# Segment maximum: two rows summed by matrix products with the identity, the maximum with zero taken in ScalarE's copy

## The chip, the core and the metric

The kernel runs on one core of a Trainium2 chip. The metric is the device time of one execution in microseconds, the median of several. A core has five engines with queues of their own: TensorE (PE, matrix products), VectorE (DVE), ScalarE (ACT), GpSimd (POOL) and SyncE (SP). DMA transfers are issued by SP, ACT and POOL. An instruction that has to wait for a semaphore holds up everything behind it on its own engine.

## The reference, cut to what matters

Four graph layers are applied to 12500 nodes of 64 features, with 400000 edges sorted by target node. The change is in the second layer, which computes an MLP on each edge and takes the maximum over the edges of each target:

```python
h = jnp.maximum(_layernorm(x, axis=-1), 0.0)
x_i = x[dst]; x_j = x[src]                     # x here is h
edge_features = jnp.concatenate([x_i, x_j - x_i], axis=-1)
h = jax.nn.relu(edge_features @ W1 + b1)
edge_messages = h @ W2 + b2
out = jax.ops.segment_max(edge_messages, dst, num_segments=x.shape[0])
```

The first product is split by linearity: every node gets one row that serves as a source (`tab1`) and one that serves as a target (`own1`, with the bias). For an edge, the hidden row is the maximum with zero of source row plus target row.

## The kernel before, in words

`target_maximum` handles the 400000 edges as 128 runs of 3125 consecutive edges, one run for each partition. It goes over them in 125 chunks (g) of 25 columns (`CB`), so a chunk is 25 edges on each partition, 128x1600 numbers. `by_columns` unrolls six chunks in a loop body; k is the place in it, so buffers are k % 2 or k % 3. Each engine runs its own list of stages, and `stage(f, lag, ...)` says which chunk a stage works on relative to g.

For a chunk:

- POOL (`gathers`) issues 25 indirect DMAs, one for each column, which bring the source rows into `G` (three buffers). Between them it issues 10 indirect DMAs that scatter records to `rec`; these belong to the later layers and only use this loop as a place to run. SP loads the source numbers (`idx`), the target rows and flags, and what the scatters need.
- ACT (`node_part`) writes target rows into `Xv`, which is laid out with features outside and columns inside (26 numbers from one feature to the next). DVE (`spread`) then carries the rows forward over the edges of one target by two scans. This is done one chunk ahead.
- DVE (`add`) sums `Xv` and `G` into `z`; ACT (`hidden`) takes the maximum with zero into `zr`.
- PE (`turn`) transposes `zr` in pairs of columns into `ps_t`, in four rounds of at most four pairs (4, 4, 4 and 1 pair; `NR2` is 4). ACT (`copies`) copies each round to `zT`, and PE (`messages`) multiplies it by the weights into `ps_m`.
- ACT (`messages`) copies `ps_m` into `Mv`, again with features outside; DVE (`scan`) takes the running maximum, and ACT (`turned`) turns it into `So`, which SP stores.

The names of instructions in the profile: `PT` is the lent memory that holds `Ein`, `G`, `Xv` and `rb`; `ACC` and `H` hold `z`, the two buffers of `zr`, and `Mv`. So "DVE ACC<-PT L1357" is the sum, "ACT ACC<-ACC L1434" and "H<-ACC L1434" are the maximum with zero. POOL's indirect DMAs have line 912 (gathers) and 891 (scatters) in this layer and in `target_attention`, the layer before it, whose loop has the same form with 15 scatters in a chunk; there the index tile is `t_idx`, here it is `m_idx`. POOL may start the gathers of chunk g when the chunk g - 3 has been read.

Of the kernel before, what the change touches and what calls it, by code (L numbers as in the profile page):

```python
# [37 lines left out]
def at_least(eng, sem, value):  # L38

    if not isinstance(value, int) or value > 0:  # L40
        eng.wait_ge(sem, value)
# [109 lines left out]
def settle(eng):  # L151


    eng.nop(nofuse=True)
# [18 lines left out]
def program(nc, x, src, dst, ea16, ea64, rowvec, wtab0, w_e, wtab1, w2, wtab2, watt_e, wgru, bgru, w1, w3, out):  # L173
# [11 lines left out]
    with ExitStack() as top:  # L185
# [713 lines left out]

            return r * (COLS_U // slots) + (k // slots + 1)  # L900

        def gathers(pool, G, table, idx, s_i, s_free, s_g, steps_in, g, k, r):

            q = k % 3
            pool.wait_ge(s_i[q], used(k, r, 3) * 16)
            at_least(pool, s_free, g - 2)
            settle(pool)
            at = {CB * (i + 1) // (steps_in.per + 1): i for i in range(steps_in.per)}
            for c in range(CB):
                if c in at:  # L910
                    steps_in.scatter(pool, at[c], k, r)
                pool.indirect_dma_start(G[:, q, c, :], None, table,  # L912
                                        bass.IndirectOffsetOnAxis(ap=idx[:, q, c:c + 1], axis=0)).then_inc(s_g[q], 16)
# [344 lines left out]
        def target_maximum():  # L1258
# [3 lines left out]
            NR2 = len(rounds)  # L1262
            with phase() as ctx:
                Mv = [hw[:, q * D * CW:(q + 1) * D * CW] for q in range(2)]
                zr = [accw[:, 2 * D * CW + CB * D:2 * D * CW + 2 * CB * D].rearrange("p (c d) -> p c d", c=CB),
                      hw[:, 2 * D * CW:2 * D * CW + CB * D].rearrange("p (c d) -> p c d", c=CB)]
                z = accw[:, 2 * D * CW:2 * D * CW + CB * D].rearrange("p (c d) -> p c d", c=CB)
                So = sb_in(ctx, "m_So", [P, 2, CB, D])
                w = sb_in(ctx, "m_w", [2 * D, 2 * D])
                zT = sb_in(ctx, "m_zT", [P, 2, 512])  # L1270
# [4 lines left out]
                ps_m = ps_in(ctx, "m_ps_m", [P, 2048])  # L1275
                ps_f = ps_in(ctx, "m_ps_f", [P, 1024])
                flags_in = ps_f[:, 0:HD * CW].rearrange("p (d c) -> p d c", c=CW)
                (s_w, s_wz, s_set, s_first, s_xv, s_F, s_Fm, s_R, s_car, s_z, s_zr, s_t, s_zT, s_msg, s_mv, s_S, s_cs, s_So) = (sem_in(ctx, "m_" + n) for n in (
                    "weights", "weights_zero", "edges_set", "first_rows", "node_rows_turned", "flags_spread", "flags_for_maxima", "node_rows_spread", "node_rows_carried",
                    "rows_added", "hidden", "hidden_turned", "hidden_copied", "messages", "messages_turned", "maxima", "maxima_carried", "maxima_turned"))  # L1280
                s_e = [sem_in(ctx, f"m_node_rows_landed{q}") for q in range(2)]
                s_f = [sem_in(ctx, f"m_flags_landed{q}") for q in range(3)]
                s_i = [sem_in(ctx, f"m_sources_landed{q}") for q in range(3)]
# [4 lines left out]
                with nc.Block() as block:  # L1288
# [34 lines left out]
                    @block.gpsimd  # L1323
                    def _(pool):
                        pool.indirect_dma_start(first_row[:], None, own1,
                                                bass.IndirectOffsetOnAxis(ap=chunk_key[:, 0:1], axis=0)).then_inc(s_first, 16)

                        def body(g, k, r):
                            gathers(pool, G, tab1, idx, s_i, s_z, s_g, fill, g, k, r)
                        by_columns(pool, NCB, body, 0)  # L1330
                        fill.landed(pool)

                    @block.vector
                    def _(dve):
                        dve.memset(w[:], 0.0).then_inc(s_wz, 1)
                        dve.memset(flags_in[:, :, 0], -FLAG).then_inc(s_set, 1)
                        dve.memset(Mv[0].rearrange("p (d c) -> p d c", c=CW)[:, :, 0], -FLAG).then_inc(s_set, 1)
                        dve.wait_ge(s_first, 16)
                        dve.tensor_copy(Xv[0].rearrange("p (d c) -> p d c", c=CW)[:, :, 0], first_row[:]).then_inc(s_set, 1)
                        dve.wait_ge(s_set, 3)  # L1340

                        def spread(g, k, r):
                            q = k % 2
                            x3 = [v.rearrange("p (d c) -> p d c", c=CW) for v in Xv]
                            dve.wait_ge(s_xv, g + 1)
                            dve.wait_ge(s_F, g + 1)
                            at_least(dve, s_car, g)
                            dve.tensor_tensor_scan(Xv[q][:, 0:HD * CW], ps_f[:, 0:HD * CW], Xv[q][:, 0:HD * CW], 0.0, ALU.add, ALU.max)
                            dve.tensor_tensor_scan(Xv[q][:, HD * CW:D * CW], ps_f[:, 0:HD * CW], Xv[q][:, HD * CW:D * CW], 0.0, ALU.add, ALU.max).then_inc(s_R, 1)
                            dve.wait_ge(s_R, g + 1)  # L1350
                            dve.tensor_copy(x3[1 - q][:, :, 0], x3[q][:, :, CB]).then_inc(s_car, 1)

                        def add(g, k, r):
                            dve.wait_ge(s_R, g + 1)
                            dve.wait_ge(s_g[k % 3], used(k, r, 3) * (16 * CB))
                            at_least(dve, s_zr, g)
                            dve.tensor_tensor(z, Xv[k % 2].rearrange("p (d c) -> p c d", c=CW)[:, 1:CW, :], G[:, k % 3], ALU.add).then_inc(s_z, 1)  # L1357

                        def scan(g, k, r):
                            q = k % 2  # L1360
                            m3 = [v.rearrange("p (d c) -> p d c", c=CW) for v in Mv]
                            dve.wait_ge(s_mv, g + 1)
                            dve.wait_ge(s_Fm, g + 1)
                            at_least(dve, s_cs, g)
                            dve.tensor_tensor_scan(Mv[q][:, 0:HD * CW], ps_f[:, 0:HD * CW], Mv[q][:, 0:HD * CW], 0.0, ALU.add, ALU.max)  # L1365
                            dve.tensor_tensor_scan(Mv[q][:, HD * CW:D * CW], ps_f[:, 0:HD * CW], Mv[q][:, HD * CW:D * CW], 0.0, ALU.add, ALU.max).then_inc(s_S, 1)
                            dve.wait_ge(s_S, g + 1)
                            dve.tensor_copy(m3[1 - q][:, :, 0], m3[q][:, :, CB]).then_inc(s_cs, 1)

                        def body(*at):  # L1370
                            stage(scan, 1, NCB, *at, unroll=COLS_U)
                            stage(spread, -1, NCB, *at, unroll=COLS_U)
                            stage(add, 0, NCB, *at, unroll=COLS_U)
                        spread(0, 0, 0)
                        by_columns(dve, NCB, body, 1)

                    @block.tensor
                    def _(pe):
                        pe.wait_ge(s_w, 32)

                        def turn(g, k, r, j):
                            at_least(pe, s_zT, g * NR2 + (j - 1))
                            settle(pe)
                            for i, pair in enumerate(rounds[j]):
                                n = 2 if 2 * pair + 1 < CB else 1
                                mm = pe.transpose(ps_t[0:n * D, j % 2, i * P:(i + 1) * P], zr[k % 2][:, 2 * pair:2 * pair + n, :], ident[:])  # L1386
                            mm.then_inc(s_t, 1)

                        def messages(g, k, r, j):
# [6 lines left out]
                            mm.then_inc(s_msg, 1)  # L1396

                        def body(g, k, r):
                            pe.wait_ge(s_zr, g + 1)
                            for j in range(NR2):  # L1400
                                turn(g, k, r, j)
                                if j == 1:
                                    at_least(pe, s_mv, g)
                                if j:
                                    messages(g, k, r, j - 1)
                            messages(g, k, r, NR2 - 1)
# [3 lines left out]
                    def _(act):  # L1410
                        def node_part(g, k, r):
                            q = k % 2
                            act.wait_ge(s_e[q], used(k, r, 2) * 16)
                            at_least(act, s_z, g - 1)
                            settle(act)
                            act.copy(Xv[q].rearrange("p (d c) -> p c d", c=CW)[:, 1:CW, :], Ein[:, q]).then_inc(s_xv, 1)

# [9 lines left out]
                            settle(act)  # L1427
                            act.copy(flags_in[:, :, 1:CW], bcast(flp[:, k % 3], 1, HD)).then_inc(s_Fm, 1)  # L1428

                        def hidden(g, k, r):  # L1430
                            act.wait_ge(s_z, g + 1)
                            at_least(act, s_t, (g - 1) * NR2)
                            settle(act)
                            act.activation(zr[k % 2], z, ACT.Relu).then_inc(s_zr, 1)  # L1434

                        def copies(g, k, r):
                            for j in range(NR2):
                                n = len(rounds[j]) * P
                                act.wait_ge(s_t, g * NR2 + (j + 1))
                                at_least(act, s_msg, g * NR2 + (j - 1))  # L1440
                                settle(act)
                                act.copy(zT[:, j % 2, 0:n], ps_t[:, j % 2, 0:n]).then_inc(s_zT, 1)

                        def messages(g, k, r):
                            q = k % 2
# [12 lines left out]
                        def body(*at):  # L1458
# [1 line left out]
                            stage(flags_again, 1, NCB, *at, unroll=COLS_U)  # L1460
                            stage(turned, 1, NCB, *at, unroll=COLS_U)
                            stage(flags, -1, NCB, *at, unroll=COLS_U)
                            stage(hidden, 0, NCB, *at, unroll=COLS_U)
                            stage(copies, 0, NCB, *at, unroll=COLS_U)
                            stage(messages, 0, NCB, *at, unroll=COLS_U)
                            stage(lambda *a: fill.keys(act, *a), -2, NCB, *at, unroll=COLS_U)
# [1052 lines left out]
```

## Time and profile before

| | |
|---|---|
| median of 3 runs | 23699.2 us (23693.9 to 23703.35) |
| the profiled execution | 23729.27 us, its span 23727.5 us |
| POOL busy | 16160.3 us, 68% of the span |
| DVE busy | 10675.2 us, 45% |
| PE busy | 8267.3 us, 35% |
| ACT busy | 6494.6 us, 27% |
| gathers of the segment maximum (L912, `m_idx`) | 3125, from 8307.2 to 14074.5 us |
| granted TensorE clock | mean 0.625 of full speed; 0.57 in this layer |

A profile gives busy times for each engine, and for each group of instructions the idle time before it and what ended that. POOL's issue of one indirect DMA counts as busy; the row's "idle before" is what lay between two of them. One POOL instruction takes about 0.95 us, so the 46 us of a chunk are the 35 of them one after another.

### The profile page before, as it was taken

What the parts mean: (1) busy time and instruction counts of PE and PEld (TensorE: products, weight loads), DVE (VectorE), ACT (ScalarE), POOL (GpSimd) and SP (SyncE); (2) the same over time, 40 slices, a digit from 0 to 9 for tenths busy, and PEclk for the clock granted to TensorE, in tenths of its full rate; (3) what the DMA queues carried; (4) which work ended last, traced back from release to release, by engine and by line L of the source; (5) the groups of instructions that cost most, each with busy time, mean ns of one, the idle gap of its engine ahead of it and who ended that gap; (6) DMA issues with size and microseconds to landing.
All of it is one profiled execution on the core that took longest, in us unless ns stands there. A gap on an engine that the chain in (4) does not pass through costs nothing. (4 is left out here: it accounts for less than half of the span.)

```text
span 23727.5 us, 309845 instructions
## 1 busy us (share of the span) xinstructions
PE 8267.3 (35%) x52022; PEld 6762.3 (29%) x52023; DVE 10675.2 (45%) x28947; ACT 6494.6 (27%) x15429; POOL 16160.3 (68%) x16650
## 2 busy tenths in 40 slices
PE   2431111111111111111111116888888753333334
PEld 1110000000000111111111115777787733333333
DVE  4744444444444322222222216777777554444445
ACT  0012222222222133333333323555555411111111
POOL 1057777777777477777777774777777527777773
PEclk7755555555555555555555557999999755555555
DMA  9223333333333122222222225777777823333333
GB/s 413 82 61 78 81 80 79 79 81 79 78 81 80 43 73 72 71 72 72 71 72 72 71 58 61 86 86 86 86 86 86 66 37 60 60 60 60 60 60 34
DMA packets 2547246, 1881.33 MB, mean 79 GB/s; under 512 B 1939077, under 2 KB 2190275, under 8 KB 2525087
## 3 DMA queue, kind: packets, MB, share of 16 engines
q1 hardware_dynamic: 1766148, 1106.93, 21.6%
q0 software_dynamic: 536736, 602.92, 15.8%
q10 hardware_dynamic: 244252, 170.38, 2.5%
q14 instruction: 85, 0.69, 0.0%
q8 instruction: 25, 0.41, 0.0%
HBM read 1244.80 MB, written 635.40 MB: 79 GB/s over the span
## 5 line engine op out<-in xcount | busy, mean ns | idle before, releaser
L1724 POOL DMA_INDIRECT H<-tab,a_rs x3520 | 3350.7, 952 | 1434.6 <-issue 970.7
L1994 POOL DMA_INDIRECT g_G<-tab,g_rs x3232 | 3065.4, 948 | 1364.6 <-issue 1000.9
L912 POOL DMA_INDIRECT PT<-tab,m_idx x3125 | 3209.2, 1027 | 955.1 <-issue 952.4
L891 POOL DMA_INDIRECT rec<-PT,posi x3125 | 3064.9, 981 | 952.9 <-issue 952.6
L912 POOL DMA_INDIRECT PT<-tab,t_idx x3125 | 2976.5, 952 | 957.8 <-issue 952.1
L1107 PE MATMUL t_ps_z<-t_w,t_eaT 128*128 128x512 f32 x1000 | 671.2, 826 | 5563.9 <-DVE ACC L1081 2789.4
L2075 PE MATMUL g_ps_a<-g_zr,g_oh 128*128 128x64 f32 x6464 | 1586.5, 427 | 2578.9 <-ACT g_zr L2056 2144.2
L2075 PEld LDWEIGHTS g_ps_a<-g_zr,g_oh 128*128 128x128 f32 x6464 | 1438.7, 327 | 2726.7 <-issue 1996.5
L1107 PEld LDWEIGHTS t_ps_z<-t_w,t_eaT 128*128 128x128 f32 x1000 | 265.7, 291 | 5987.9 <-issue 5984.8
L1042 DVE TENSOR_TENSOR t_ps_z<-t_ps_z,PT 128x1600 f32<-128x1600 f32 x125 | 229.1, 1833 | 3256.9 <-DMA PT<-tab,t_idx 3256.9
L2024 DVE TENSOR_TENSOR ACC<-ACC,g_ps_a 128x64 f32 x3232 | 715.5, 221 | 1925.7 <-DVE ACC L2024 1550.0
L1357 DVE TENSOR_TENSOR ACC<-PT 128x1600 f32<-128x1600 f32 x125 | 396.8, 3174 | 1858.2 <-DMA PT<-tab,m_idx 1858.2
L1828 PE MATMUL a_ps_z<-a_w_in,a_gT 81*128 81x144 f32 x7040 | 1176.6, 315 | 29.8 <-DVE a_z L1749 25.3
L1143 ACT ACTIVATE ACC<-t_ps_z 128x1600 f32<-128x1600 f32 x125 | 188.0, 1504 | 3629.1 <-DVE t_ps_z L1042 3629.1
L1365 DVE TENSOR_TENSOR_SCAN H<-m_ps_f,H 128x832 f32<-128x832 f32 x125 | 236.3, 1891 | 2058.4 <-ACT m_ps_f L1428 2058.4
L1386 PE MATMUL m_ps_t<-ident,ACC 128*128 128x128 f32 x819 | 194.9, 394 | 2493.1 <-ACT ACC L1434 2493.1
L1828 PEld LDWEIGHTS a_ps_z<-a_w_in,a_gT 81*128 81x128 f32 x7040 | 1017.6, 208 | 98.2 <-DVE a_z L1749 44.4
L1386 PE MATMUL m_ps_t<-ident,H 128*128 128x128 f32 x806 | 195.0, 399 | 2416.0 <-ACT H L1434 2416.0
L1757 DVE TENSOR_SCALAR H<-iota_b,a_lo,a_p 128x128 f32<-128x128 bf16 x3520 | 998.7, 363 | 23.5 <-ACT a_p L1929 23.0
L1835 PE MATMUL a_ps_z<-PT,a_ohN 128*128 x10560 | 998.5, 244 | 0.8 <-issue 0.5
L1859 PE MATMUL a_ps_a<-H 128*128 128x65 f32 x7040 | 994.0, 286 | 1.0 <-DVE H L1757 1.0
L1770 DVE CUSTOM_DVE_ANT_0 a_junk<-a_ps_lb,a_pen,a_mo 128x512 bf16<-128x512 f32 x880 | 660.5, 751 | 700.2 <-PE a_ps_lb L1844 474.3
(423 smaller groups left out, 23574.2 us busy)
## 6 DMA issues: line engine op xcount, KB each, us to landing
PT<-expand SPq DMA_DIRECT2D x250, 800.0 KB, 4.5
rec<-H SPq DMA_DIRECT2D x88, 1640.0 KB
a_rs<-rec SPq DMA_DIRECT2D x880, 164.0 KB
a_row<-keyc SPq DMA_DIRECT2D x880, 128.0 KB
sums<-t_So SPq DMA_DIRECT2D x125, 850.0 KB
expand<-H ACTq DMA_DIRECT2D x80, 1250.0 KB
PT<-in_ea SPq DMA_DIRECT2D x625, 160.0 KB
maxima<-m_So SPq DMA_DIRECT2D x125, 800.0 KB
```

Of the source, the lines that this page charges most:

```text
L891: pool.indirect_dma_start(rec, bass.IndirectOffsetOnAxis(ap=self.posi[:, q, t:t + 1], axis=0), rbi[:, q, t, :], None).then_inc(self.s_sc[q ...
L912: pool.indirect_dma_start(G[:, q, c, :], None, table, bass.IndirectOffsetOnAxis(ap=idx[:, q, c:c + 1], axis=0)).then_inc(s_g[q], 16)
L1107: mm = pe.matmul(ps_z[:, c * D:(c + n) * D], eaT[0:n * DE, t * P:(t + 1) * P], w[0:n * DE, 0:n, :].rearrange("p t c -> p (t c)"), start=Tr ...
L1724: pool.indirect_dma_start(G[:, k, t, 0:D], None, tab3, bass.IndirectOffsetOnAxis(ap=rs[:, k, t, 1:2], axis=0)).then_inc(s_g[k], 16)
L1757: ins = dve.tensor_scalar(oh[:, k % SLOTS, t, :], iota_b[:], lo[:, k, t:t + 1], p[:, t:t + 1], ALU.is_equal, ALU.mult)
L1770: dve.tensor_tensor_reduce(junk[:], ps_lb[:], pen[:, k % 2], 1.0, mo[:, k % 2:k % 2 + 1], ALU.add, ALU.max, mn[:]).then_inc(s_mn, 1)
L1828: pe.matmul(zv[b][:, t % tpb, :], gT[:, k % 2, t * P:(t + 1) * P], w[:], start=(t % tpb == 0), stop=False)
L1835: mm = pe.matmul(zv[t // tpb][:, t % tpb, :], ohN[:, k % SLOTS].rearrange("n (p t) -> n t p", t=T)[:, t, :], PT[:, bass.ds(blk_g, 1), i, 0 ...
L1859: mm = pe.matmul(ps_a[:, k % 2, 0:VC], oh[:, k % SLOTS, t, :], G[:, k, t, 0:VC], start=(t == 0), stop=(t == T - 1))
L1994: pool.indirect_dma_start(G[:, k, t, :], None, tab3, bass.IndirectOffsetOnAxis(ap=rs[:, k, t, 1:2], axis=0)).then_inc(s_g[k], 16)
L2024: dve.tensor_tensor(acc, acc, ps_a[:, k % 2, t, 0:D], ALU.add).then_inc(s_done, 1)
L2075: mm = pe.matmul(ps_a[:, q, t, 0:D], oh[:, q, t, :], zr[:, q, t, :], start=True, stop=True)
```

## The change

`add` and `hidden` are gone, and with them the buffers `z` and `zr`. `turn` on PE now does three matrix products for a pair of columns, with the identity as the moving operand and into the same 128x128 part of `ps_t`: one with the two gathered columns as the stationary operand, and one for each of the two columns of `Xv`, which is added to 64 of the 128 partitions. ACT's `copies` takes the maximum with zero as it copies. PE itself now waits for the node rows and for the gathered rows. POOL and `node_part` wait for PE's count of rounds in place of DVE's count of chunks (hence `per`), and `node_part` also for the carry.

```diff
-            at_least(pool, s_free, g - 2)
+            at_least(pool, s_free, (g - 2) * per)
...
-                        def add(g, k, r):
-                            dve.wait_ge(s_R, g + 1)
-                            dve.wait_ge(s_g[k % 3], used(k, r, 3) * (16 * CB))
-                            at_least(dve, s_zr, g)
-                            dve.tensor_tensor(z, Xv[k % 2].rearrange("p (d c) -> p c d", c=CW)[:, 1:CW, :], G[:, k % 3], ALU.add).then_inc(s_z, 1)
...
-                                mm = pe.transpose(ps_t[0:n * D, j % 2, i * P:(i + 1) * P], zr[k % 2][:, 2 * pair:2 * pair + n, :], ident[:])
+                                to = ps_t[0:n * D, j % 2, i * P:(i + 1) * P]
+                                pe.matmul(to, G[:, k % 3, 2 * pair:2 * pair + n, :], ident[:], start=True, stop=False)
+                                for c in range(n):
+                                    mm = pe.matmul(to[c * D:(c + 1) * D], xv[k % 2][:, 1 + 2 * pair + c, :], ident[:], start=False, stop=True)
...
-                            pe.wait_ge(s_zr, g + 1)
+                            pe.wait_ge(s_R, g + 1)
+                            settle(pe)
+                            pe.wait_ge(s_g[k % 3], used(k, r, 3) * (16 * CB))
+                            settle(pe)
...
-                            at_least(act, s_z, g - 1)
+                            at_least(act, s_t, (g - 1) * NR2)
+                            settle(act)
+                            at_least(act, s_car, g - 1)
...
-                        def hidden(g, k, r):
-                            act.wait_ge(s_z, g + 1)
-                            at_least(act, s_t, (g - 1) * NR2)
-                            settle(act)
-                            act.activation(zr[k % 2], z, ACT.Relu).then_inc(s_zr, 1)
...
-                                act.copy(zT[:, j % 2, 0:n], ps_t[:, j % 2, 0:n]).then_inc(s_zT, 1)
+                                act.activation(zT[:, j % 2, 0:n], ps_t[:, j % 2, 0:n], ACT.Relu).then_inc(s_zT, 1)
```

On PE, in one chunk of the segment maximum, before:

```order
L1386 MATMUL m_ps_t<-ident,ACC 128x128 x8
L1394 MATMUL m_ps_m<-m_w,m_zT 128x128 x4
L1386 MATMUL m_ps_t<-ident,ACC 128x128 x4
L1394 MATMUL m_ps_m<-m_w,m_zT 128x128 x4
L1386 MATMUL m_ps_t<-ident,ACC 64x128
L1394 MATMUL m_ps_m<-m_w,m_zT 128x128 x4
L1394 MATMUL m_ps_m<-m_w,m_zT 128x64
```

and with the change, from the end of the second round on (`PT` is `G` in line 1378 and `Xv` in line 1380):

```order
L1378 MATMUL m_ps_t<-ident,PT 128x128
L1380 MATMUL m_ps_t<-ident,PT 64x128 x2
L1388 MATMUL m_ps_m<-m_w,m_zT 128x128 x4
L1378 MATMUL m_ps_t<-ident,PT 128x128
L1380 MATMUL m_ps_t<-ident,PT 64x128 x2
L1378 MATMUL m_ps_t<-ident,PT 128x128
L1380 MATMUL m_ps_t<-ident,PT 64x128 x2
L1378 MATMUL m_ps_t<-ident,PT 128x128
L1380 MATMUL m_ps_t<-ident,PT 64x128 x2
L1378 MATMUL m_ps_t<-ident,PT 128x128
L1380 MATMUL m_ps_t<-ident,PT 64x128 x2
L1388 MATMUL m_ps_m<-m_w,m_zT 128x128 x4
```

Thirteen transposes of a chunk became 13 + 25 products, and the message products stand where they stood.

On ACT, in one chunk, before:

```order
L1434 ACTIVATE ACC<-ACC 128x1600
L1442 COPY m_zT<-m_ps_t 128x512 x3
L1442 COPY m_zT<-m_ps_t 128x128
L1449 COPY H<-m_ps_m 128x25x64
L882 CAST PT<-PT 128x5x2
```

and with the change:

```order
L1435 ACTIVATE m_zT<-m_ps_t 128x512 x3
L1435 ACTIVATE m_zT<-m_ps_t 128x128
L1442 COPY H<-m_ps_m 128x25x64
L882 CAST PT<-PT 128x5x2
```

One instruction of 128x1600 left ACT and one (L1357) left DVE; nothing else changed its place.

## Rows read from the trace of the kernel before

**Rows 1.** The page: busy time by engine, granted TensorE clock in 40 slices.
```profile
PE 8267.3 (35%) x52022; PEld 6762.3 (29%) x52023; DVE 10675.2 (45%) x28947; ACT 6494.6 (27%) x15429; POOL 16160.3 (68%) x16650
...
PEclk7755555555555555555555557999999755555555
```

**Rows 2.** Groups by shape, 8300 to 14160 us: busy, mean ns | idle before, releasers.
```profile
L912 POOL DMA_INDIRECT PT<-tab,m_idx x3125 | 3209.2, 1027 | 955.1 <-issue 952.4 <-DMA m_idx<-in_src 2.7
L891 POOL DMA_INDIRECT rec<-PT,posi x1250 | 1225.6, 980 | 381.1 <-issue 380.8 <-DMA rec<-PT,posi 0.3
...
L1456 ACT COPY m_So<-H 128x1600 f32<-128x1600 f32 x125 | 399.9, 3199 | 487.9 <-DVE H L1366 487.9
...
L1357 DVE TENSOR_TENSOR ACC<-PT 128x1600 f32<-128x1600 f32 x125 | 396.8, 3174 | 1858.2 <-DMA PT<-tab,m_idx 1858.2
...
L1348 DVE TENSOR_TENSOR_SCAN PT<-m_ps_f,PT 128x832 f32<-128x832 f32 x125 | 236.3, 1891 | 487.6 <-ACT m_ps_f L1423 487.6
...
L1434 ACT ACTIVATE ACC<-ACC 128x1600 f32<-128x1600 f32 x63 | 96.8, 1536 | 1405.1 <-DVE ACC L1357 1405.1
...
L1351 DVE COPY PT<-PT 128x64 f32<-128x64 f32 x125 | 30.9, 247 | 4.3
...
L1386 PEld LDWEIGHTS m_ps_t<-ident,ACC 128*64 128x64 f32 x63 | 7.4, 117 | 0.0
```

**Rows 3.** The same view of the layer before, 1500 to 8290 us.
```profile
L912 POOL DMA_INDIRECT PT<-tab,t_idx x3125 | 2976.5, 952 | 957.8 <-issue 952.1 <-DMA t_idx<-in_src 5.4 <-DMA PT<-in_ea 0.3
...
L1039 DVE TENSOR_TENSOR t_ps_z<-t_ps_z,PT 128x1600 f32<-128x1600 f32 x125 | 397.4, 3180 | 198.2 <-PE t_ps_z L1107 198.2
```

**Rows 4.** Tile `m_idx`: duration in ns min/median/max, first and last start.
```profile
L912 POOL DMA_INDIRECT PT<-tab,m_idx x3125: 941/947/3893, 8307.2 to 14074.5; - x196
```

**Rows 5.** Timeline of one chunk's sum: start, duration, engine, line [idle before].
```profile
11031.67 0.95 POOL L912 DMA_INDIRECT PT<-tab,m_idx  x1 [0.30 <-issue]
11031.72 3.17 DVE L1357 TENSOR_TENSOR ACC<-PT 128x1600 f32<-128x1600 f32 x1 [14.05 <-DMA PT<-tab,m_idx]
11031.89 0.35 SPq L1298 DMA_DIRECT2D m_idx<-in_src  x1
...
11032.92 2.74 POOL L912 DMA_INDIRECT PT<-tab,m_idx  x1 [0.30 <-issue]
...
11035.96 0.95 POOL L912 DMA_INDIRECT PT<-tab,m_idx  x1 [0.31 <-issue]
```

**Rows 6.** Timeline in the layer before: a load by SP, and a sum.
```profile
5008.09 0.35 SPq L973 DMA_DIRECT2D t_idx<-in_src  x1
...
5009.13 0.94 POOL L912 DMA_INDIRECT PT<-tab,t_idx  x1 [0.30 <-issue]
...
5030.23 3.17 DVE L1039 TENSOR_TENSOR t_ps_z<-t_ps_z,PT 128x1600 f32<-128x1600 f32 x1 [2.33 <-PE t_ps_z L1107]
5030.75 0.97 POOL L891 DMA_INDIRECT rec<-PT,posi  x1 [0.30 <-issue]
```

**Rows 7.** Timeline of PE in one chunk.
```profile
11082.79 1.94 PE L1386 MATMUL m_ps_t<-ident,H 128*128 128x128 f32 x8 [38.96 <-ACT H L1434]
11084.77 2.04 PE L1394 MATMUL m_ps_m<-m_w,m_zT 128*128 128x128 f32 x8
...
11089.18 1.42 PE L1394 MATMUL m_ps_m<-m_w,m_zT 128*128 128x128 f32 x10
```

**Rows 8.** Timeline: ScalarE and VectorE behind PE's work on a chunk.
```profile
11043.94 3.15 ACT L1449 COPY H<-m_ps_m 128x1600 f32<-128x1600 f32 x1 [1.07 <-PE m_ps_m L1394]
...
11062.76 0.23 DVE L1351 COPY PT<-PT 128x64 f32<-128x64 f32 x1
```

**Rows 9.** Timeline of the layer's end.
```profile
14076.92 3.17 DVE L1357 TENSOR_TENSOR ACC<-PT 128x1600 f32<-128x1600 f32 x1 [25.46 <-DMA PT<-tab,m_idx]
...
14087.18 1.49 PE L1394 MATMUL m_ps_m<-m_w,m_zT 128*128 128x128 f32 x10
...
14099.83 0.33 SPq L1311 DMA_DIRECT2D maxima<-m_So  x1
```

More of the change, by code:

```diff
@@ L900, in used, with gathers @@
             return r * (COLS_U // slots) + (k // slots + 1)
-        def gathers(pool, G, table, idx, s_i, s_free, s_g, steps_in, g, k, r):
+        def gathers(pool, G, table, idx, s_i, s_free, s_g, steps_in, g, k, r, per=1):
             q = k % 3
             pool.wait_ge(s_i[q], used(k, r, 3) * 16)
-            at_least(pool, s_free, g - 2)
+            at_least(pool, s_free, (g - 2) * per)
             settle(pool)
@@ L1264, in target_maximum @@
                 Mv = [hw[:, q * D * CW:(q + 1) * D * CW] for q in range(2)]
-                zr = [accw[:, 2 * D * CW + CB * D:2 * D * CW + 2 * CB * D].rearrange("p (c d) -> p c d", c=CB),
-                      hw[:, 2 * D * CW:2 * D * CW + CB * D].rearrange("p (c d) -> p c d", c=CB)]
-                z = accw[:, 2 * D * CW:2 * D * CW + CB * D].rearrange("p (c d) -> p c d", c=CB)
                 So = sb_in(ctx, "m_So", [P, 2, CB, D])
@@ L1277, in target_maximum @@
                 flags_in = ps_f[:, 0:HD * CW].rearrange("p (d c) -> p d c", c=CW)
-                (s_w, s_wz, s_set, s_first, s_xv, s_F, s_Fm, s_R, s_car, s_z, s_zr, s_t, s_zT, s_msg, s_mv, s_S, s_cs, s_So) = (sem_in(ctx, "m_" + n) for n in (
+                (s_w, s_wz, s_set, s_first, s_xv, s_F, s_Fm, s_R, s_car, s_t, s_zT, s_msg, s_mv, s_S, s_cs, s_So) = (sem_in(ctx, "m_" + n) for n in (
                     "weights", "weights_zero", "edges_set", "first_rows", "node_rows_turned", "flags_spread", "flags_for_maxima", "node_rows_spread", "node_rows_carried",
-                    "rows_added", "hidden", "hidden_turned", "hidden_copied", "messages", "messages_turned", "maxima", "maxima_carried", "maxima_turned"))
+                    "rows_added_turned", "hidden_copied", "messages", "messages_turned", "maxima", "maxima_carried", "maxima_turned"))
                 s_e = [sem_in(ctx, f"m_node_rows_landed{q}") for q in range(2)]
@@ L1328, in body @@
                         def body(g, k, r):
-                            gathers(pool, G, tab1, idx, s_i, s_z, s_g, fill, g, k, r)
+                            gathers(pool, G, tab1, idx, s_i, s_t, s_g, fill, g, k, r, NR2)
                         by_columns(pool, NCB, body, 0)
@@ L1372, in body @@
                             stage(spread, -1, NCB, *at, unroll=COLS_U)
-                            stage(add, 0, NCB, *at, unroll=COLS_U)
                         spread(0, 0, 0)
@@ L1379, in _ @@
                         pe.wait_ge(s_w, 32)
+                        xv = [v.rearrange("p (d c) -> p c d", c=CW) for v in Xv]
                         def turn(g, k, r, j):
@@ L1462, in body @@
                             stage(flags, -1, NCB, *at, unroll=COLS_U)
-                            stage(hidden, 0, NCB, *at, unroll=COLS_U)
                             stage(copies, 0, NCB, *at, unroll=COLS_U)
```

## The prediction

> **What bounds the kernel now.** I read the page first: POOL has the largest share, 68% of the span [rows 1], and no engine is near full over the whole, so each layer must be read by itself. The groups of the segment maximum come next. There POOL does two things, 3125 gathers and 1250 scatters. Their busy time and the idle time before them add up to 3209.2 + 955.1 + 1225.6 + 381.1 = 5771 us [rows 2], and the gathers run from 8307.2 to 14074.5 us, 5767 us [rows 4]. So POOL fills the stretch by itself, and its idle time is the fixed 0.30 us of issue between two instructions; it waits for nobody but once, 2.7 us at the start. The chunk of 46.2 us (5771 / 125) is POOL's. DVE's sum waits 1858.2 us for gathered rows, ACT's maximum with zero waits 1405.1 us for the sum [rows 2]: both have room. Taking 3.17 us off DVE and 1.54 us off ACT per chunk therefore gives nothing by itself. What matters is whether POOL's own instructions get shorter or longer.
>
> **What POOL loses now.** The same gather costs 1027 ns on average here [rows 2] and 952 ns in the layer before [rows 3], with equal count. The median here is 947 ns and the longest 3893 ns [rows 4]: a few instructions are long, not all a little. The timeline shows which. The sum on DVE starts at 11031.72 and ends at 11034.89; the gather that starts at 11032.92, inside it, takes 2.74 us and ends at 11035.66, 0.77 us after the sum's end, and the next one takes 0.95 again [rows 5]. I read this as a lock-out: POOL stops while the sum runs and does the rest of its 0.95 us behind it. The sum always starts when the last gather of the chunk before has landed, so one gather per chunk is always hit. The stretches I read show one long gather for each sum and none elsewhere.
>
> The layer before separates two suspects. There SP also issues loads just as the rows have landed (5008.09), and the gather beside them takes 0.94 us. There is also a DVE sum of the same length, 3.17 us at 5030.23, and the POOL instruction inside it takes 0.97 us [rows 6]. That sum has one operand in PSUM; the sum of the segment maximum has both in SBUF. The scans (L1348) too take one from PSUM, and run beside POOL without a long instruction. So the two SBUF operands of L1357 are what stops POOL.
>
> The Trainium skill, page "SBUF — State Buffer", section "Who interferes with whom", says that a VectorE instruction with two SBUF inputs blocks a GpSimd instruction that reads SBUF until it is done. The same section also infers that writing descriptors needs only the other, write side, and that a `tensor_tensor` therefore does not stall a GpSimd DMA. By the first rule the stall goes with the sum; by the second it was never the sum's, and the time stays near 23,704 us (the second rival below). Rows 5 and 6 together speak for the first.
>
> **The change part by part.**
>
> 1. The sum leaves DVE. From the equal counts, POOL's excess is 3209.2 - 2976.5 = 232.7 us [rows 2, 3]. From the median it is 3209.2 - 3125 x 0.947 = 249.8 us [rows 2, 4]. I take 240 us, 1.9 us in each chunk. All of it is on the path, since POOL fills the stretch. The chunk becomes 44.25 us. Nothing that DVE keeps has two large SBUF inputs.
>
> 2. The maximum with zero leaves ACT, and its copies become activations of the same shape. ACT had room and keeps it: nothing.
>
> 3. PE. Before, a chunk had 13 transposes of one record each and 13 message products of two records each (four pairs stand as x8 [rows 7]), 39 records. Now the 38 products of `turn` take two records each if fp32 products are like the messages, so 76 + 26 = 102. Eight cost 2.04 us early in a burst and ten cost 1.42 us at its end [rows 7], 0.255 us and 0.142 us each. The granted clock of this layer's slices is mostly 5 tenths [rows 1]; I read the first price as the 1.2 GHz level and the second as partly or wholly the 2.4 GHz level, reached some 6 us into a burst that followed 39 us of idle PE. All slow, 102 records are 26.0 us; all fast, 14.5 us. Behind a start of 6 us with 24 slow records, 78 x 0.142 = 11.1 us, together 17 us; I take 17.
>
> 4. Is PE hidden? Behind PE's work, ACT and DVE need from 11043.94 to 11062.99, 19 us, before ACT can copy for the next chunk [rows 8]. 17 + 19 = 36 us stay under 44.25. Even 26 + 19 = 45 does not bind, because PE can do the first two rounds of the next chunk (48 of the 102 records) before ACT copies anything. So PE's work is hidden, by POOL's 44 us, and only the very last chunk pays for it.
>
> 5. The strided operand. `Xv` is read with 26 numbers between neighbours, and no row shows PE reading so. ACT reads such a tile in 3199 ns and a dense one of the same size in 1536 ns [rows 2], 2.1 times. A dense load of 64 columns takes 117 ns [rows 2], so 0.24 us strided, no more than the slow record that I already bounded by 0.255. Below, the cost is nothing, since weight loads lie beside products. I take nothing for it.
>
> The skill's page "SBUF — State Buffer", section on the DMA port swizzle, says that SBUF is read in 16-byte lines and that each access to a new line pays a penalty, with four fp32 numbers as the dense reach. It gives no figure for PE. This rule speaks against the change, since every number of `Xv` lies on a line of its own; the sum would be the same as long as a record stays under the limit in the third rival.
>
> 6. The new waits. PE waits for the gathered rows itself; behind it stand only products of that chunk. POOL's wait for chunk g - 3 now ends with the last `turn` of it, some 10 us later than the sum did, while two whole chunks (88 us) lie between. `node_part` waits for `turn` of two chunks before, also long done. The extra register step on POOL, once in a chunk, has the 0.30 us issue gap to hide in: 0 to 125 x 0.05 = 6 us, taken as nothing.
>
> 7. The end of the layer. PE now starts at the landing, where the sum started (14076.92), and PE's last record ended at 14088.67, 11.8 us later [rows 9]. With 17 us it is 5 us later; with 14.5 to 26 it is 3 to 14.
>
> Sum against the profiled execution: 23729.3 - 240 + 5 = 23494 us. The median of the runs lies 30 us under that execution, so 23464 us, 1.0% faster.
>
> **The rivals.**
>
> - Part of it comes back. DVE keeps two copies of 128x64 per chunk from SBUF to SBUF (L1351, and L1368 of the same shape), 0.25 us each [rows 2]. No long gather shows beside them now, but if they began to stop POOL fully in the shorter chunk, 125 x 2 x 0.25 = 62 us return: 23526 us. A new wait of half a microsecond on POOL per chunk would do the same. Against it: POOL has run past these copies at every phase already.
>
> - The stall is not the sum's but comes with the landing (SP's seven loads fall in the same 4 us), or the change does not free POOL for another reason. Then only the 5 us at the end remain: 23704 us, no change. For it: the coincidence in rows 5. Against: rows 6.
>
> - Slower: PE becomes the bound through the strided weight loads. With the other 52 records at the slow 0.255 us, PE alone fills 44.25 us when 52 x 0.255 + 50 x s = 44.25, so from s = 0.62 us per `Xv` record. At three times the slow record, 0.765 us, a chunk takes 51.5 us, 5.3 us more than the 46.2 of before: + 660 us, 24,360 us. Against it: the 2.1 of ACT gives 0.24 us, under half of that limit.
>
> **How the numbers follow.** The forecast of 23464 has 87%, the part return 5%, no change 5%, slower 3%. What a measurement of this kernel can tell from no change is about 0.2%, 47 us. The first two cases are both faster by more. The forecast's own range is -250 + 3 to -233 + 14 + 6, so 23452 to 23486; I widen it by some 12 us down for run-to-run difference, and up to the part return: 23440 to 23530.
>
> **What would show it.** In the profile after, the gather's mean must fall from 1027 to about 950 ns with the longest near 1.0 us; its first and last start must lie 5527 us apart instead of 5767; POOL's idle must still be "issue" alone. PE's bursts must last 14 to 26 us and start at the landing, and the store of the last chunk some 5 us later behind the last gather. The prediction is wrong if long gathers remain without the sum (second rival), if POOL's gathers wait for `m_ps_t`, or if ACT's copies and PE leave no idle time in a chunk (third).

## The result, and the profile after

| | before | after |
|---|---|---|
| median, the same chip | 23701.28 us, 4 runs | 23985.77 us, 4 runs (23959.43 to 24004.5) |
| profiled execution | 23729.27 us | 23959.43 us, span 23957.7 us |

The ratio is 1.012, 95% interval 1.0102 to 1.0137: 1.2% slower, where 1.0% faster was forecast. The median also lies outside the forecast range of 23440 to 23530 us. The profiled execution is the fastest of the four, so the two profiles differ by 230 us and the two medians by 284; the account below is of the profiles.

In the segment maximum it went as forecast. This is the tile `m_idx` (columns as in [rows 4]):

```profile
L912 POOL DMA_INDIRECT PT<-tab,m_idx x3125: 940/944/1035, 8295.2 to 13813.0; - x196
```

In [rows 4] the longest gather took 3893 ns and the first and last start were 5767.3 us apart. Now the longest takes 1035 ns and they are 5517.8 us apart, 249.5 us less. The groups by shape, 8290 to 13900 us, answer to [rows 2]:

```profile
L912 POOL DMA_INDIRECT PT<-tab,m_idx x3125 | 2962.7, 948 | 954.7 <-issue 952.0 <-DMA m_idx<-in_src 2.7
L891 POOL DMA_INDIRECT rec<-PT,posi x1250 | 1223.1, 978 | 381.0 <-issue 380.7 <-DMA rec<-PT,posi 0.3
...
L1380 PE MATMUL m_ps_t<-ident,PT 128*64 128x128 f32 x6250 | 1033.8, 417 | 0.0
...
L1435 ACT ACTIVATE m_zT<-m_ps_t 128x512 f32<-128x512 f32 x375 | 223.9, 597 | 3096.8 <-PE m_ps_t L1380 3096.8
```

The mean of a gather fell from 1027 to 948 ns, and POOL still waits for nothing but issue.

The loss comes later, in code that the change doesn't touch. `source_attention` has POOL's gathers `a_rs`, 3520 of them. Before:

```profile
L1724 POOL DMA_INDIRECT H<-tab,a_rs x3520: 939/947/1225, 14451.5 to 19017.5; - x196
```

and after (each line 8 lower, since the file is 8 lines shorter there):

```profile
L1716 POOL DMA_INDIRECT H<-tab,a_rs x3520: 938/944/1109, 14195.5 to 19262.4; - x196
```

Each gather takes the same, but the stretch grew from 4566.0 to 5066.9 us, by 500.9. The account of the two profiled executions: 12.0 us less up to the first `m_idx`, 249.5 less there, 5.5 more to the first `a_rs`, 500.9 more in it, 14.7 less behind it: 230.2 us more, which is the difference of the spans.

Who is late there is told by DVE's waits (total us, times, longest), 14400 to 18600 us, before:

```profile
DVE a_junk L1770 <- PE a_ps_lb L1844: 442.7, 312, 9.5
DVE a_dd L1777 <- PE a_ps_m L1851: 255.2, 769, 1.7
DVE a_z L1749 <- issue: 163.7, 677, 0.6
```

and after:

```profile
DVE a_z L1741 <- issue: 840.3, 663, 9.8
DVE a_dd L1769 <- PE a_ps_m L1843: 243.4, 729, 1.6
DVE a_junk L1762 <- PE a_ps_lb L1836: 231.7, 265, 3.2
```

"issue" is time in which no semaphore was waited for, and its longest went from 0.6 to 9.8 us. DVE's timeline after shows one such place:

```profile
15058.44 0.28 DVE L1780 SCALAR_TENSOR_TENSOR ACC<-ACC,a_corr,a_ps_a 128x65 f32 x1
15059.01 0.16 DVE L1769 TENSOR_TENSOR a_dd<-a_lg,a_ps_m 128x4 f32<-128x4 f32 x1 [0.29 <-PE a_ps_m L1843]
15059.20 0.17 DVE L1772 TENSOR_SCALAR a_dd<-a_dd 128x4 f32<-128x4 f32 x1
15067.61 0.31 DVE L1741 SCALAR_TENSOR_TENSOR a_z<-a_ps_z,rows 128x144 bf16<-128x144 f32 x1 [8.23 <-issue]
```

The groups around it take 4 to 6 us each and have 0.19 us in that place. Such a stall comes once in a pass of the loop, which handles 8 of the 880 groups. The first and the last 8 groups stand outside the loop, so it has 108 passes and 107 jumps back to its start. Over the whole layer DVE's idle time ahead of `a_z` put down to issue grew from 174.0 to 1032.1 us, 8.0 us for each jump. PE and ACT then wait for `a_z`: the PE group L1820 has 870.6 us of idle time put down to it, 25.3 before. Not all of the 858 us reach the stretch, which grew by 501: DVE waits less for PE elsewhere, as the rows of `a_junk` show.

A further line of the page changed, the queue that brings instructions. Before:

```profile
q14 instruction: 85, 0.69, 0.0%
```

and after (packets, MB, share):

```profile
q14 instruction: 618, 5.06, 0.1%
```

These are 533 more packets of 8 KB. The full list of records in the trace tells where they fall. In both programs DVE has 108 branch records in the layer, 310 records apart, with waits and branches counted. Between each two of them five packets of 8 KB come on this queue in the kernel after, 107 times out of 107, and none in the kernel before. The first record behind the branch follows it by 5.05 us in the median, 0.22 before. So DVE's loop is fetched anew in every pass. Its text is the same in both programs. What changed is where it lies: `add` had 12 records ahead of the segment maximum's loop, 14 in its body and 22 behind it, so DVE's program is 48 records shorter ahead of the loop in `source_attention`.

### The profile page after: what moved, and what is told of

Its sections match the earlier page's. It is cut to its first block and busy times, and to the rows that moved or that the text cites. A ratio compares the mean times of both kernels' runs of the same rounds, so it can differ in the third digit from the quotient of the medians.

```text
span 23957.7 us, 325485 instructions
## 1 busy us (share of the span) xinstructions
PE 9944.4 (42%) x59897; PEld 7705.2 (32%) x59898; DVE 10254.5 (43%) x28822; ACT 6293.7 (26%) x15304; POOL 15877.8 (66%) x16650
## 5 line engine op out<-in xcount | busy, mean ns | idle before, releaser
L912 POOL DMA_INDIRECT PT<-tab,m_idx x3125 | 2962.7, 948 | 954.7 <-issue 952.0
L1378 PE MATMUL m_ps_t<-ident,PT 128*128 128x128 f32 (+1 forms) x3250 | 1135.0, 447 | 3058.4 <-DMA PT<-tab,m_idx 3058.4
L1378 PEld LDWEIGHTS m_ps_t<-ident,PT 128*128 128x128 f32 (+1 forms) x3250 | 722.7, 278 | 3441.9 <-issue 3399.1
L1820 PE MATMUL a_ps_z<-a_w_in,a_gT 81*128 81x144 f32 x7040 | 1237.5, 325 | 874.8 <-DVE a_z L1741 870.6
L1820 PEld LDWEIGHTS a_ps_z<-a_w_in,a_gT 81*128 81x128 f32 x7040 | 1042.4, 213 | 980.4 <-DVE a_z L1741 899.0
L1741 DVE SCALAR_TENSOR_TENSOR a_z<-a_ps_z,rows 128x144 bf16<-128x144 f32 x3520 | 872.4, 304 | 1046.4 <-issue 1032.1
L1435 ACT ACTIVATE m_zT<-m_ps_t 128x512 f32<-128x512 f32 x500 | 258.5, 517 | 3249.1 <-PE m_ps_t L1380 3249.1
L1380 PE MATMUL m_ps_t<-ident,PT 128*64 128x128 f32 x6250 | 1033.8, 417 | 0.0
```

Of the source, the lines that this page charges most:

```text
L912: pool.indirect_dma_start(G[:, q, c, :], None, table, bass.IndirectOffsetOnAxis(ap=idx[:, q, c:c + 1], axis=0)).then_inc(s_g[q], 16)
L1378: pe.matmul(to, G[:, k % 3, 2 * pair:2 * pair + n, :], ident[:], start=True, stop=False)
L1380: mm = pe.matmul(to[c * D:(c + 1) * D], xv[k % 2][:, 1 + 2 * pair + c, :], ident[:], start=False, stop=True)
L1741: ins = dve.scalar_tensor_tensor(z[:, t, :], zv[t // tpb][:, t % tpb, :], 0.0, att, ALU.max, ALU.mult, accum_out=ss[:, t:t + 1])
L1820: pe.matmul(zv[b][:, t % tpb, :], gT[:, k % 2, t * P:(t + 1) * P], w[:], start=(t % tpb == 0), stop=False)
```

## The experiments

They were of two kinds: removing the stall of the gathers without the change, and moving DVE's loop of `source_attention` without touching it. One more moves ScalarE's program instead. The moves of DVE's loop are made by small memsets of spare columns, added to DVE's program behind the segment maximum's loop. One takes 59 ns, and even 204 of them start between 14112.3 and 14117.8 us and run once.

**48 memsets behind the change** (`after_dve48`)

```diff
                         by_columns(dve, NCB, body, 1)
+                        for i in range(48):
+                            dve.memset(spare1[:, i:i + 1], 0.0)
```

> The changed kernel with 48 tiny memsets added on VectorE behind the last scan of the segment maximum, so that VectorE's code of the layer behind it stands where it stood before the change (the sum's removal had moved it up by 48 instructions). Theory, code fetch: VectorE's loop in source_attention (310 records a pass in both traces) costs a wait of 8 to 10 us once a pass only because of where it stands. The waits 'DVE a_z <- issue' fall back from 9.8 us at most to 0.6 us, the instruction queue q14 from 618 packets to about 85, the layer from 5063 us to about 4566 us, and the time is 23,701 - 250 + 10 = about 23,461 us. Rival: PE's longer program, the granted clock or the timing that the segment maximum leaves behind slows the layer; then 48 memsets on VectorE change nothing and the time stays near 23,985 us.

Measured: 23451.78 us (23443.64 to 23453.2) beside 23686.48 for the kernel before: 0.9899 (0.9883 to 0.9916). Its tile rows and queue:

```profile
L912 POOL DMA_INDIRECT PT<-tab,m_idx x3125: 940/944/1039, 8289.5 to 13807.1; - x196
L1719 POOL DMA_INDIRECT H<-tab,a_rs x3520: 938/944/1113, 14192.1 to 18754.1; - x196
```

```profile
q14 instruction: 84, 0.69, 0.0%
```

and DVE's waits in the layer:

```profile
DVE a_z L1744 <- issue: 165.9, 690, 0.6
```

`a_rs` takes 4562.0 us again and the stall is gone. With 48 useless instructions the change is worth the 1.0% that was forecast.

**204 memsets in the kernel before** (`before_dve204`), in the same place:

> The kernel before, with nothing of the change, and 204 tiny memsets on VectorE at the same place. Theory, code fetch: a shift of the loop alone brings the fault into the kernel before. One wait of 8 to 10 us in each of some 108 passes, q14 over 600 packets, source_attention some 490 us longer, time about 24,190 us plus some 10 us for the memsets. Rival (PE's program or timing): 23,701 us plus at most 12 us for the memsets. The count of 204 is chosen by the Trainium skill, page 'Runtime: NRT & Kernel Launch', section 'Instruction fetch mechanics': blocks of 256 instructions, of which two are held, so a loop of 310 that touches three blocks is fetched again on every pass; 204 leads there from every start that fits both traces.

24165.93 us, 1.0198 (1.0181 to 1.0215).

```profile
L1727 POOL DMA_INDIRECT H<-tab,a_rs x3520: 938/947/1113, 14464.1 to 19494.5; - x196
```

```profile
q14 instruction: 620, 5.08, 0.1%
```

```profile
DVE a_z L1752 <- issue: 776.5, 728, 7.5
```

So the loss appears without the change, by the position alone: `a_rs` takes 5030.4 us. The 204 came from a model of two blocks of 256 instructions, which the runs further down refute; that it hit is partly luck.

**The same 48 on ScalarE** (`after_act48`): `act.copy(spare1[:, i:i + 1], pcol[:])`, behind ScalarE's loop.

> The changed kernel with 48 tiny copies on ScalarE instead, some 10 us of ScalarE at the segment maximum's end. Theory, code fetch on VectorE: nothing changes but those few us; the waits 'DVE a_z <- issue' stay at 8 to 10 us, q14 stays near 618 packets, time 23,960 to 24,010 us. Rival: any shift of code or of time breaks up the slow pattern; then near 23,465 us.

23984.75 us in one run, 619 packets, as after. Moving ScalarE's program by 48 changes nothing.

**The sum without two SBUF operands** (`before_psum`). This kernel leaves the gathered rows in `G` out of the sum; it reads as many zeros from PSUM in their place, and it also waits for the copy out of `ps_m`.

```diff
+                        dve.memset(ps_m[:, 0:CB * D], 0.0).then_inc(s_set, 1)
...
-                            dve.tensor_tensor(z, Xv[k % 2].rearrange("p (d c) -> p c d", c=CW)[:, 1:CW, :], G[:, k % 3], ALU.add).then_inc(s_z, 1)
+                            at_least(dve, s_mv, g)
+                            dve.tensor_tensor(z, ps_m[:, 0:CB * D].rearrange("p (c d) -> p c d", c=CB), Xv[k % 2].rearrange("p (d c) -> p c d", c=CW)[:, 1:CW, :], ALU.add).then_inc(s_z, 1)
```

> The kernel before with one operand of VectorE's sum in the segment maximum taken from PSUM (m_ps_m in place of the gathered rows, so the sum leaves the gathered rows out); the sum keeps its place, its size, its strided second operand and its wait for the gathered rows. Theory, lock-out by two SBUF operands: the gather under the sum is no longer long; mean of L912 on m_idx from 1027 ns to about 950, longest near 1.0 us, time 23,701 - 240 = about 23,461 us. Rival: the long gather comes with the landing and with SP's loads that fall there; the mean stays 1027 ns and the time 23,701 us.

23441.13 us, 0.9894 (0.9878 to 0.9911). Its groups by shape in the layer:

```profile
L912 POOL DMA_INDIRECT PT<-tab,m_idx x3125 | 2962.7, 948 | 954.6 <-issue 952.0 <-DMA m_idx<-in_src 2.7
...
L1359 DVE TENSOR_TENSOR ACC<-m_ps_m,PT 128x1600 f32<-128x1600 f32 x125 | 394.2, 3154 | 1613.8 <-DMA PT<-tab,m_idx 1613.8
```

The sum still takes 3154 ns and still starts at the landing of the rows, and the gathers take 948 ns. So it is the second SBUF operand that stops POOL, and neither the sum's length nor its moment. This operand was also the buffer of the gathered rows. Whether reading just that buffer matters, and not the count of SBUF operands, was not tested apart.

**How few are enough** (`after_dve12`, `after_dve24`, `after_dve36`; one run each, beside 23695.31 us for the kernel before):

> The changed kernel with 12 memsets on VectorE in place of 48. Theory, whole blocks of code: VectorE's loop either needs a fetch on every pass or on none, so with 0 to 48 memsets there is one edge, and this run is wholly slow (q14 about 620 packets, about 23,985 us) or wholly fast (q14 about 85, about 23,455 us); three runs of 12, 24 and 36 place the edge within 12 instructions. Rival, a cost that falls little by little with the distance: a time between, near 23,850 us, and a q14 count between.

> The changed kernel with 24 memsets on VectorE. Theory, whole blocks: wholly slow (q14 about 620, about 23,985 us) or wholly fast (q14 about 85, about 23,455 us), and fast if 12 is fast. Rival, a gradual cost: near 23,720 us.

> The changed kernel with 36 memsets on VectorE. Theory, whole blocks: wholly slow (q14 about 620, about 23,985 us) or wholly fast (q14 about 85, about 23,455 us), and fast if 24 is fast. Rival, a gradual cost: near 23,590 us.

23441.68, 23483.73 and 23448.02 us, with 83, 84 and 84 packets. Even 12 are enough.

**Which blocks** (`before_dve60`, `before_dve150`, `before_dve170`, `after_dve6`). Two models stood against each other, blocks of 256 instructions of which two stay loaded, and blocks of 128. If three blocks of 128 stay loaded, a loop of 310 is in trouble where it touches four: at 53 starts of every 128 (310 = 384 - 74), with the same pattern 128 further on. The expectations were written with the blocks of 256.

> The kernel before with 60 memsets on VectorE. The edge lies between 0 and 12 memsets in the changed kernel, that is 36 to 47 instructions above the loop's place in the kernel before. If code is held in blocks of 256 instructions, two at a time, a loop of 310 is slow from 53 places before such an edge up to it; 60 memsets stand clear of the next one: q14 about 85, about 23,695 us. Rival, blocks of 128 instructions (each q14 packet carries 8 KB): the next edge is 128 further, 60 memsets lie in front of it by 21 to 32 instructions, so the loop is slow: q14 over 600, about 24,170 us.

> The kernel before with 150 memsets on VectorE. Blocks of 256 instructions, two held: the slow places begin at 156 to 167 memsets, so this is still fast: q14 about 85, about 23,700 us. If the loop needs more room than its 310 records (instructions that leave no record), or the blocks are held otherwise, it is slow already: q14 over 600, about 24,170 us.

> The kernel before with 170 memsets on VectorE. Blocks of 256 instructions, two held, 310 records in the loop: just inside the slow places, which begin at 156 to 167: q14 over 600, about 24,170 us. If the slow stretch is shorter than the 53 places that 310 records give, it is fast: q14 about 85, about 23,705 us.

> The changed kernel with 6 memsets on VectorE: it halves the place of the edge, which lies between 0 and 12. Wholly slow (about 23,985 us, q14 about 620) or wholly fast (about 23,455 us, q14 about 85). Nothing between is expected by the theory; a gradual cost would give near 23,700 us.

These four ran once each, on a chip on which the kernel before itself took 28735.88 us. Their packets can still be counted:

| kernel | place of the loop against before | packets | us on that chip |
|---|---|---|---|
| before_dve60 | +60 | 620 | 28972.0 |
| before_dve150 | +150 | 86 | 28737.63 |
| before_dve170 | +170 | 620 | 28917.85 |
| after_dve6 | -42 | 83 | 29319.62 |

`before_dve60` was expected to keep its loop by the blocks of 256, and it was refetched, as its rival with blocks of 128 had it. With the earlier ones: refetched at -48, +60, +170 and +204, kept at -42, -36, -24, -12, 0 and +150. Modulo 128 that is 80, 60, 42, 76 against 86, 92, 104, 116, 0, 22, so the refetched places form one unbroken stretch in a circle of 128. In a circle of 256 they form two: 60, then kept at 150, refetched from 170 to 208, kept from 214. `before_psum`, whose extra waits and memset move the loop by 21, kept it too. One thing stays open: four touched blocks would make four packets in a pass, and there are five.

The Trainium skill, page "Runtime: NRT & Kernel Launch", section "Instruction fetch mechanics", gives the instruction memory as two blocks of 16 KiB, 256 instructions each, and says that a taken branch out of the two forces a fetch. As an estimate from these figures, a packet of 8 KB holds 128 instructions, and a loop of 310 would be in trouble at 53 starts of every 256. The runs show packets of 8 KB and a second stretch, and they decide. What it says of the branch agrees with the trace, the 5.05 us behind the branch.

**The last steps once more** on a chip of the usual kind (`tel_dve6`, `tel_dve48`, `tel_psum` and `tel_dve150` are `after_dve6`, `after_dve48`, `before_psum` and `before_dve150` once more, beside 23708.09 us for the kernel before):

> The kernel after with 6 memsets on VectorE behind the loop of the segment maximum. On a chip on which the kernel before takes about 23700 us: 23450 us by the theory that 6 instructions are enough to move VectorE's loop of the source attention into three blocks (83 to 86 packets on the instruction queue); 23960 us and about 619 packets by the rival that more than 6 are needed. On a chip on which it takes near 29000 us: a ratio of 1.02, as in two looks.

> The kernel after with 48 memsets in the same place. On a chip of about 23700 us: 23450 us again. On a chip near 29000 us: a ratio of 1.02 if the new order of the segment maximum is what is slower there (its gathers of m_idx over 7000 us in all); 0.99 to 1.00 if it was the place of the code with 6 memsets.

> The kernel before with the add reading a cleared PSUM bank instead of the gathered rows, which it leaves out of the sum. On a chip of about 23700 us: 23440 us again. On a chip near 29000 us: about 0.99 to 1.00 if the cost there lies in the new chain of PE and ScalarE ahead of the sum (this one keeps the old order), 1.02 if lifting the lock-out itself brings it (earlier gathers that collide with other transfers).

> The kernel before with 150 memsets on VectorE behind the loop, which move the source attention's loop past a whole block and leave it loaded: the same time as the kernel before on either kind of chip, 83 to 86 packets on the instruction queue. The rival, that any instructions added there cost in the loops behind them: 1.01 or more.

| kernel | us | ratio, 95% interval | packets |
|---|---|---|---|
| tel_dve6 | 23473.52 | 0.99 (0.9881 to 0.9919) | 83 |
| tel_dve48 | 23472.35 | 0.99 (0.988 to 0.9919) | 84 |
| tel_psum | 23452.94 | 0.9893 (0.9874 to 0.9913) | 85 |
| tel_dve150 | 23708.48 | 1.0 (0.999 to 1.0011) | 86 |

Six memsets repair the change, and 150 in the kernel before cost nothing, so it is not that added instructions cost by themselves.

**On a chip of the slower kind** (`after_dve6_again`):

> The kernel after with 6 small memsets on VectorE behind the loop of the segment maximum, once more, since its one look fell in a call in which the kernel before itself took 28736 us. Theory (the cost is where VectorE's loop of the source attention lies, 6 instructions move it into three blocks): about 23450 us, ratio 0.990 to the kernel before, 83 to 86 packets on the instruction queue, VectorE's idle time ahead of a_z about 0.66 us. Rival A (fewer than about 12 instructions aren't enough, and the earlier look had other reasons for its few packets): 23960 us, about 619 packets. Rival B (the change is slower by itself, as the one look of 29320 us beside 28736 has it): a ratio of 1.02, with gathers of m_idx that take over 6000 us in all.

This was again such a chip: 29574.12 us beside 28957.28, ratio 1.0215 (1.0196 to 1.0234), with 83 packets. Rival B held there. POOL's waits in the segment maximum, 8990 to 16150 us:

```profile
POOL rec L891 <- issue: 1286.3, 1196, 23.4
POOL PT L912 <- issue: 951.7, 3123, 0.3
POOL rec L891 <- ACT posi L883: 713.6, 54, 13.3
```

and in `before_dve150`, on the other such chip, 8980 to 15540 us:

```profile
POOL rec L891 <- issue: 1074.3, 1250, 13.6
POOL PT L912 <- issue: 952.4, 3124, 0.3
```

ScalarE makes `posi`, behind its copies of `m_zT` and `m_ps_m`. Its waits, `after_dve6_again` first:

```profile
ACT m_zT L1438 <- DMA own<-staged_row: 4605.4, 128, 38.7
```

```profile
ACT m_zT L1445 <- DMA own<-staged_row: 1421.8, 77, 29.4
```

From first to last start the gathers of `m_idx` take 7136.6 us, against 6519.7. `after_dve6`, which ran on the chip of `before_dve150`, has 7124.6: 604.9 us more, where the two kernels differ by 582. So on that chip the whole loss lies in the segment maximum, and with 83 packets none of it comes from refetching.

The releaser named in the last two rows misleads. `own<-staged_row` are 98 stores of earlier stages, the last at 8973.0 us. In the code these copies wait only for PE, for its rounds of `turn` and its message products. The view falls back on an older user of the same semaphore when a signal comes long after the end of PE's records. So it is PE's signals that are late. In `after_dve6_again` the copy of the third or the fourth round of a chunk starts more than 5 us behind the end of that round's last PE record in 245 of 250 cases, some 30 us in the median. In `before_dve150` it does so in 124 of 250, and in `after` and `before` in none; there the copy follows within 0.4 us.

POOL doesn't fill the stretch by itself on such a chip even before: it has 1074.3 us of issue time ahead of the scatters where [rows 2] have 380.8. With the change it also waits 713.6 us for `posi`, which stands behind the late copies on ScalarE. My reading is that PE finishes late on these chips, and that the change, which gives PE 102 records in a chunk in place of 39, puts more work behind it. That is argued from these rows and not shown: the version with 48 memsets and the one without the sum's second SBUF operand never ran on such a chip. Why PE is late there stays open.

## Why the prediction was wrong

The step that failed is the last one, the sum 23729.3 - 240 + 5, by what it leaves out; its two terms hold. What failed in it is the unstated premise that everything outside the segment maximum keeps its time. "The change part by part" has no term for the code behind it; the missing term is +501 us in `source_attention`, by 48 records fewer ahead of DVE's loop. With it the sum is 23729.3 - 240 + 5 + 501 = 23995 us; the profiled execution was 23959.43 us. The way from the profiled execution to the median failed too, by 56 us: it was taken as 30 us down, and the median lies 26 us above. None of the three rivals has the missing term. That nothing else changed its place, as the section on the change has it, was true of the order and not of the addresses.

- What bounds the kernel, and the lock-out: right. `before_psum` removes it alone and gains 245 us, as the change with 48 memsets gains 235. Of the two rules on two SBUF inputs that the prediction sets against each other, the first held for these indirect DMAs.
- Step 1 (DVE's sum, 240 us): right, 249.5, the upper of the two bounds of the estimate.
- Step 2 (ScalarE, nothing): right, 597 ns for a copy of 512 columns, with 3096.8 us of waiting for PE.
- Step 3 (PE's burst of 17 us, 14.5 to 26): it took 19.8 us. PE after, in one chunk:

```profile
11034.09 0.77 PE L1378 MATMUL m_ps_t<-ident,PT 128*128 128x128 f32 x2 [24.43 <-DMA PT<-tab,m_idx]
11034.79 0.70 PE L1380 MATMUL m_ps_t<-ident,PT 128*64 128x128 f32 x4
11035.42 0.80 PE L1378 MATMUL m_ps_t<-ident,PT 128*128 128x128 f32 x2
...
11048.59 0.50 PE L1380 MATMUL m_ps_t<-ident,PT 128*64 128x128 f32 x4
11049.02 0.49 PE L1378 MATMUL m_ps_t<-ident,PT 128*128 128x128 f32 x2
11049.44 0.50 PE L1380 MATMUL m_ps_t<-ident,PT 128*64 128x128 f32 x4
11049.87 0.49 PE L1378 MATMUL m_ps_t<-ident,PT 128*128 128x128 f32 x2
...
11052.39 1.52 PE L1388 MATMUL m_ps_m<-m_w,m_zT 128*128 128x128 f32 x10
```

  A pair of columns, six records, comes every 1.36 us at the start and every 0.85 us at the end: 0.227 and 0.142 us a record. So the slow record is cheaper than my 0.255, but the short ones begin only some 14 us into the burst, not 6, and 17 us was 2.8 us too low.
- Step 4 (PE hidden): right on the usual chips; PE waits 3058.4 us for gathered rows over the layer, 24.5 us a chunk. On the slower chips PE's signals come late and POOL waits behind them.
- Step 5 (strided operand, nothing): right. From start to start, the four strided records of a pair take 0.63 us at the beginning of the burst (11034.79 to 11035.42), 0.16 us each, and the two dense ones from `G` the rest of the 1.36. The limit was 0.62 us for one; the slower rival through PE is out.
- Step 6 (new waits, nothing): right on the usual chips; POOL has 0.3 us as its longest wait in the loop. On the slower chips POOL waits for `posi`, 713.6 us in all.
- Step 7 (end of layer, +5 us): the last store starts 33.8 us behind the last gather's start, 25.3 before, so 8.5 us later, within the 3 to 14 that were given. The first `a_rs` comes 5.5 us later (382.5 against 377.0).
- The second rival (no change) is dead. The first (62 us come back) didn't happen: the gain was whole.

The chance of 0.92 for faster was too high for a reason that can be named: I went through every engine and wait in the changed layer and took the other layers' time over unread. A removal of instructions ahead of a long loop is a change to that loop.

## What to carry to other kernels

When a change adds or removes instructions ahead of an unrolled loop, look at the instruction queue's packets and at long "issue" waits in loops that the change doesn't touch: here 85 packets became 618 and one such wait in each pass grew to some 8 us, and with six memsets the same change was 1.0% faster instead of 1.2% slower. A loop that has nearly the size of what stays loaded (here 310 records, where the runs fit 384) should be shortened or placed on purpose. And a VectorE sum of two SBUF operands can hold up a stream of GpSimd's indirect DMAs: here each sum of 3.17 us cost the stream 2.0 us (249.5 / 125), and with one operand in PSUM nothing. Last, measure on more than one chip where PE takes over work: on the slower chips used here the same change, with its loop kept loaded, lost 2%.

## What the hardware showed

- VectorE's instructions come in packets of 8 KB, and the runs fit blocks of 128 instructions with three held. A loop of 310 that touches a fourth is fetched with five packets in every pass, where a loop kept loaded has none, and 8 groups that took 41.5 us (4566.0 / 110) take 46.1.
- The identity products of the burst got the shorter records some 14 us in, after 24 us of idle PE; the burst before got them some 6 us in, after 39 us [rows 7]. In `source_attention` the granted clock fell with the stalls. The stretch 15000 to 16000 us before (us, PE, PEld, DVE, ACT, POOL busy, clock, DMA share, GB/s):

```profile
15000.00:16000.00 1000.00, 883.67 (x7958) 789.45 (x7956) 724.89 (x3589) 524.99 (x2192) 757.54 (x796) 0.94 0.75 86
```

  and the same stage after:

```profile
14770.00:15770.00 1000.00, 818.95 (x7132) 731.56 (x7132) 647.75 (x3214) 467.82 (x1961) 675.62 (x713) 0.87 0.64 78
```

  PE worked less and its clock fell from 0.94 to 0.87, between its two levels of 1.2 and 2.4 GHz. PE's busy time for one record rose from 0.111 to 0.115 us. With 48 memsets the clock is 0.94 again.
- Two chips of those used here ran the kernel before in 28736 and 28957 us. POOL issues a gather in the same 0.944 or 0.947 us (median) there, and PE's signals come late (above). On such a chip a change can have the other sign.
